# Graph convolutions: 28 of 56 tiles gathered and seven groups picked, in place of 24 and eight, with the scan's flags in PSUM

## What is computed

```python
edge_index = jnp.stack([src, dst])
x = _layernorm(x + L0(x, edge_attr_16, ...))    # edge softmax over incoming edges
x = _layernorm(x + L1(x, edge_type_8, ...))     # two relational convolutions
x = _layernorm(x + L2(x, edge_attr_8, ...))     # message and update products
x = _layernorm(x + L3(x, edge_attr_8, ...))     # three edge-conditioned convolutions

# one relational convolution (L1)
msg = sum over r of where(edge_type == r, x[src] @ W[r], 0)
out = segment_sum(msg * norm[:, None], dst) + x @ root + bias

# one edge-conditioned convolution (L3)
W = (edge_attr @ ew + eb).reshape(E, 16, 16)
msg = einsum('ei,eio->eo', x[src], W)
out = segment_sum(msg, dst) + x @ rw + rb
```

## Time and profile before

| | us |
|---|---|
| median of three runs | 13711.05 (13693.49 to 13768.67) |
| profiled execution, own time | 13760.25 |
| its span | 13759.0 |
| stretch of r0 | 1150 |
| stretch of r1 | 1368 |
| stretches of c0, c1, c2 | 1490, 1512, 1503 |
| granted TensorE clock, mean | 0.786 |

### The profile page before, as it was taken

The page is one execution under the profiler, slowest core; times in us unless marked ns, Lnnn a source line. Parts: engine busy times, 40 slices in busy tenths (PEclk is TensorE's granted clock), DMA queues, the critical chain, the costliest instruction groups (busy, mean ns, idle before and its releaser), DMA issues. The chain is left out here.

```text
span 13759.0 us, 163456 instructions
## 1 busy us (share of the span) xinstructions
PE 10347.0 (75%) x42305; PEld 7078.4 (51%) x42305; DVE 9334.6 (68%) x14722; ACT 8279.7 (60%) x16314; POOL 7292.7 (53%) x6233
## 2 busy tenths in 40 slices
PE   6888888888724887687748888777775777767775
PEld 2333333333313665565537777655554555545554
DVE  8999999999878776343349999545554454535454
ACT  5777777777623665465538887455553555535553
POOL 4555555555653776555457776344443444444444
PEclk7666666666657998798879999788886888778887
DMA  3444444444434776465521111266664666546663
GB/s 129 176 177 177 176 179 178 177 176 176 159 125 170 255 255 214 140 205 184 187 62 46 45 45 44 58 207 212 206 210 127 203 203 203 190 138 213 202 207 124
DMA packets 750356, 2256.00 MB, mean 164 GB/s; under 512 B 272537, under 2 KB 420654, under 8 KB 673806
## 3 DMA queue, kind: packets, MB, share of 16 engines
q10 hardware_dynamic: 161280, 1027.68, 21.8%
q1 hardware_dynamic: 388638, 984.49, 19.0%
q0 software_dynamic: 200304, 242.20, 8.0%
HBM read 1321.84 MB, written 931.93 MB: 164 GB/s over the span
## 5 line engine op out<-in xcount | busy, mean ns | idle before, releaser
L592 POOL DMA_INDIRECT h<-in_x,idx x1568 | 2055.3, 1311 | 1699.8 <-DMA efT<-in_edge_attr_t 1245.4
L676 ACT ACTIVATE PX<-PX,h 128x16 f32<-128x16 f32 x12544 | 2513.1, 292 | 23.0 <-issue 13.8
L1474 PE MATMUL PS<-every_weight,dstf 112*128 112x144 f32 (+1 forms) x8960 | 1444.3, 302 | 625.7 <-DVE dstf L1606 387.5
L1474 PEld LDWEIGHTS PS<-every_weight,dstf 112*128 112x128 f32 x8960 | 1338.8, 206 | 843.4 <-DVE dstf L1606 409.0
L625 PE MATMUL PS<-M,minus_ident 128*128 128x512 f32 x1568 | 1410.2, 1025 | 310.0 <-DVE M L710 310.0
L1992 PE MATMUL PS<-mhr,lhs 128*128 128x392 f32 x6272 | 1264.6, 358 | 204.1 <-DVE lhs L2156 193.1
L1959 POOL DMA_INDIRECT myg<-node_table,mix x784 | 1099.9, 1403 | 458.7 <-issue 247.0
L2055 ACT ACTIVATE mhr<-mhb 128x1568 fp32r<-128x1568 bf16 x784 | 1142.2, 1505 | 302.6 <-DVE mhb L2146 251.9
L1992 PEld LDWEIGHTS PS<-mhr,lhs 128*128 128x128 f32 x6272 | 1151.9, 194 | 291.8 <-ACT mhr L2055 141.1
L613 PE MATMUL PS<-waug,efT 17*128 17x256 f32 x6272 | 1038.7, 534 | 283.4 <-DVE e L688 247.7
L1452 POOL DMA_INDIRECT c0yg<-node_table,c0ix x672 | 686.1, 1021 | 950.6 <-DVE c0run L1675 555.3
(11 more groups left out here) (419 smaller groups left out, 20474.8 us busy)
## 6 DMA issues: line engine op xcount, KB each, us to landing
softmax_maxima<-M SPq DMA_DIRECT2D x196, 1024.0 KB
softmax_denominators<-ST SPq DMA_DIRECT2D x196, 1024.0 KB
softmax_numerators<-ST SPq DMA_DIRECT2D x196, 1024.0 KB
one_hot_rows_of_sources<-r0hb ACTq DMA_DIRECT2D x224, 896.0 KB
r1hb<-one_hot_rows_of_sources ACTq DMA_DIRECT2D x224, 896.0 KB
c0hb<-one_hot_rows_of_sources ACTq DMA_DIRECT2D x224, 896.0 KB
c1hb<-one_hot_rows_of_sources ACTq DMA_DIRECT2D x224, 896.0 KB
c2hb<-one_hot_rows_of_sources ACTq DMA_DIRECT2D x224, 896.0 KB
```

Source lines behind the costliest of these rows:

```text
L592: PO.indirect_dma_start(h[b.k][:, at(q), :], None, io["x"], bass.IndirectOffsetOnAxis(ap=idx[b.k][:, q:q + 1], axis=0))\
L676: act = S.activation(PX[b.k][:, 1, t, D * i:D * i + D], PX[b.k][:, 0, t, D * i:D * i + D], ACT.Copy, scale=h[b.k][:, t, i:i + 1])
L1474: mm = PE.matmul(weighed(q)[:, r, 0:R * D], mx[q % (1 + LAG)][:, 128 * r:128 * r + 128], every[0:A9 * D, 0:R, :].rearrange("p r o -> p (r ...
```

## The change

NG goes from 24 to 28 and HG from 8 to 7, so a block has 28 gathered tiles and 28 picked ones. With it:

- c0 to c2 scale seven groups of gathered tiles instead of six. The first round of `halve` goes over seven tiles at a time (eight pieces a block) instead of eight (seven pieces); in r0 and r1 it stays at four pieces, of seven tiles instead of eight.
- In c0 to c2 DVE calls `add_both` four times a step instead of three, in two pairs, and `mask` stands between the pairs instead of behind them. The messages of the first 28 tiles are k = 14, in step 3.
- `kp`, the scan's flags, is one array in PSUM banks 2 and 3 instead of two in SBUF. `keeps` now waits for the scan of the block before instead of the one before that.
- As HG is odd, PSUM banks, `hot_` and `mx` alternate by a running count (`turn_of`, `masked`). Buffer 3 of the ring is used once a block, and its load for the next block goes ahead of those of buffers 0 to 2.
- The stored one-hot rows are contiguous for each group.
- In r0 the one-hots of a block fill three and a half buffers, and are spread as four a step.

```diff
-NG, HG = 24, 8
+NG, HG = 28, 7
-            NSC, NTR = (6, 13) if both else (0, 6)
+            NSC, NTR = (7, 14) if both else (0, 6)
...
-                    kp.append(sb(f"{name}kp{k}", [CH, D, TBC], F32, L))
+                    kp.append(PS[0:CH, 2:4, :].rearrange("p b c -> p (b c)")[:, 0:D * TBC].rearrange("p (f t) -> p f t", f=D))
...
+            def turn_of(b, q):
+                return (b.k * HG + q) % 2
+
+            def masked(b, q):
+                return mx[(b.k * HG + q) % (1 + LAG)]
...
             def rows(b, half, from_):
-                return from_[some(b, NG + 16 * half, 16), :].rearrange("(a t) c -> a (t c)", a=1).to_broadcast([128, 2048])
+                n = min(16, NPK - 16 * half)
+                return from_[some(b, NG + 16 * half, n), :].rearrange("(a t) c -> a (t c)", a=1).to_broadcast([128, 128 * n])
...
-                if due(n := groups(b, q - 3)):
+                if due(n := groups(b, (-2, -1, 0, -3, 1, 2, 3)[q])):
                     S.wait_ge(*h_cv.at(n))
...
                 def keeps(b):
-                    if due(n := b.on(-2).count(1, 1)):
+                    if due(n := b.on(-1).count(1, 1)):
...
-                            load_rows(nx, p + 4)
+                            load_rows(nx, (4, 5, 6, HG + 3, HG, HG + 1, HG + 2)[p])
...
-                    at = 1024 * (j % 2)
+                    at, n2 = 1024 * (j % 2), min(2, HG - 2 * j)
...
-                    if nx and n < 3 + p % 2:
-                        one_hot(nx, (p + 3) // 2 if p % 2 else (p + 2) // 2, n if p % 2 else 4 + n)
+                    if nx:
+                        one_hot(nx, (11 + 4 * p + n) // KT, (11 + 4 * p + n) % KT)
...
-                    if k < 6:
+                    if k < 7:
                         scale_gathered(b, k)
...
+                            halve(b, slice(t0 + 7 * n, t0 + 7 * n + 7), 4 * D)
...
-                        if b:
-                            if both:
-                                add_both(b, 3 * p)
-                            else:
-                                add_typed(b, p)
+                        if b and both:
+                            add_both(b, 4 * p)
+                            add_both(b, 4 * p + 1)
+                        elif b:
+                            add_typed(b, p)
                         one_hots(nx, p, 1)
-                        if b and both:
-                            add_both(b, 3 * p + 1)
+                        if both and nx:
+                            mask(nx, p)
                         one_hots(nx, p, 2)
                         if b and both:
-                            add_both(b, 3 * p + 2)
+                            add_both(b, 4 * p + 2)
+                            add_both(b, 4 * p + 3)
```

More of the change, by code:

```diff
@@ L1369, in conv @@
             sums_c = sums[0:E, :].rearrange("(p t) f -> p t f", p=CH)
-            KEPT = 16 * sum(kept(q) for q in TWO)
+            PER = (32, 32, 32, 16)
             def groups(b, more):
@@ L1499, in stored_rows @@
             def stored_rows(b, q):
-                rows = hots_d[bass.ds(b.i * HG + (b.k * (HG // 2) + q // 2), 1), :, q % 2, :, :]
+                rows = hots_d[bass.ds(b.i * (2 * HG) + (b.k * HG + q), 1), :, :, :]
                 return rows.rearrange("a p c e -> (a p) c e")
             def keep_rows(b, q):
-                if make and kept(q):
+                if make:
                     S.dma_start(stored_rows(b, q), hb[q // 2][:, q % 2, :, :]).then_inc(h_ld[q // 2].sem, 16)
@@ L1510, in load_rows @@
                     b, q = b.on(1), q - HG
-                if make or not kept(q) or not b.exists():
+                if make or not b.exists():
                     return
-                if due(n := groups(b, q - 3)):
+                if due(n := groups(b, (-2, -1, 0, -3, 1, 2, 3)[q])):
                     S.wait_ge(*h_cv.at(n))
@@ L1518, in widen @@
                 def widen(b, q):
-                    if make or not kept(q):
+                    if make:
                         S.wait_ge(*h_oh.at(b.count(4 * KT, KT * (q // 2) + KT)))
                     else:
-                        S.wait_ge(*h_ld[q % 4].at(b.count(32, 16 * (q // 4) + 16)))
+                        S.wait_ge(*h_ld[q % 4].at(b.count(PER[q % 4], 16 * (q // 4) + 16)))
                     if due(n := groups(b, q - 1)):
                         S.wait_ge(*h_g.at(n))
-                    S.activation(hot_[q % 2][:, :, :], hb[q // 2 if make else q % 4][:, q % 2 if make else 0, :, :], ACT.Copy)\
+                    S.activation(hot_[turn_of(b, q)][:, :, :], hb[q // 2 if make else q % 4][:, q % 2 if make else 0, :, :], ACT.Copy)\
                         .then_inc(h_cv.sem, 1)
@@ new lines, in add_both @@
+                    elif k < 23:
+                        half, n = (k - 7) // 8, (k - 7) % 8
+                        done, t0 = 7 * half, 28 * half
+                        if n < 4:
+                            if half == 0:
+                                V.wait_ge(*c_sc.at(b.count(NSC, min(2 * n + 2, 7))))
+                            else:
+                                V.wait_ge(*c_pr.at(groups(b, min(2 * n + 2, HG))))
+                            halve(b, slice(t0 + 7 * n, t0 + 7 * n + 7), 4 * D)
+                        elif n < 6:
+                            V.wait_ge(*c_tr.at(b.count(NTR, done + 2 * n - 6)))
+                            halve(b, slice(t0 + 14 * n - 56, t0 + 14 * n - 42), 2 * D)
+                        elif n == 6:
+                            V.wait_ge(*c_tr.at(b.count(NTR, done + 6)))
+                            halve(b, slice(t0, t0 + 28), D)
+                        else:
+                            V.wait_ge(*c_tr.at(b.count(NTR, done + 7)))
+                            if half == 0:
+                                run_free(b)
+                            else:
+                                V.wait_ge(*c_al.at(groups(b, HG)))
+                            ts = slice(t0, t0 + 28)
+                            V.tensor_tensor(by_feature(b, ts), y[:, ts, 0:D], y[:, ts, 8 * D:], ALU.add).then_inc(c_msg.sem, 1)
+                    elif k == 23:
@@ L1689, in add_typed @@
                     elif k < 5:
-                        V.wait_ge(*c_pr.at(groups(b, 2 * k)))
-                        halve(b, slice(8 * k - 8, 8 * k), 4 * D)
+                        V.wait_ge(*c_pr.at(groups(b, min(2 * k, HG))))
+                        halve(b, slice(7 * k - 7, 7 * k), 4 * D)
                     elif k < 7:
@@ L1816, in whole @@
                     of.base += 16 * NBC
-                for of in h_ld:
-                    of.base += 32 * NBC
+                for of, per in zip(h_ld, PER):
+                    of.base += per * NBC
                 for of in c_g:
```

92 lines of the change are left out of this document (33 added, 59 removed).

## The result

The changed kernel takes 14,308.9 us (median of four, 14,292 to 14,387) beside 13,731.6 us for the kernel before: 1.043 times as long, interval 1.040 to 1.046. I had forecast 13,913 us and a range up to 14,130. The profiled execution took 14,319.9 us, 560 more than that of before. About an hour after E1 to E4 and on another chip, the same two kernels took 12,229.5 and 11,632.9 us, 1.051 (1.050 to 1.053). E12 and E13 show why.

What follows compares the result with a forecast made beforehand. No engine is always busy; PE loses about 20 us a block while POOL gathers. c0 to c2 +156, r1 -30, r0 +91, ends -15: +202 on 13,760 us, median 13,913 us (+1.5%), own range 13,790 to 14,060, wider 13,560 to 14,130.

Steps and rivals of the forecast that it cites:

- Bursts: c0 to c2: a block's run of gathers, 28 after the change, 35.8 us; POOL then waits in a gap.
- second kind: c0 to c2: blocks whose next mask comes behind the gathers; 55.5 us against 55.2, three blocks of four.
- the ends: r1 and c0 to c2: two blocks without gathers save a group each, four more gathers precede each: -15 us.
- The step from the scan's hold to the mix: c0 to c2: without the scan delaying gathers, more blocks get their mask late: 54.5 us, +2.0 a block, +156 us.
- fixed stall: Rival: what holds PE costs a fixed 20 us a block, however many gathers; 13,332 us, chance 0.14.
- PE further: Rival: PE gets further while POOL gathers without the scan's help; 13,559 us, chance 0.12.
- Five microseconds of burst cancel a group of 4.2 almost exactly: c0 to c2: longer gathering offsets the group removed; blocks 55.5 against 55.2 us, or 51.5 against 51.6.
- first kind: c0 to c2: blocks with a mask still inside the gathers, 27 to 30 us after their start; 51.5 against 51.6 us.
- PE needs only 7 x 4.2 = 29 us and cannot be the limit unless it crawls: r0: POOL's time alone sets the stage, 41.4 us a block against 38; +91 us.
- r0 falls into r1's pattern: Rival: DVE, waiting for rows, no longer slows r0's gathers; 48 us a block, +196, 14,096 us and up; chance 0.10.
- five masks fall in the first 22 us as now: r1: mask times in the gathers stay, sixth at 40 us; 47.5 us a block against 48.5, stage -30 us.
- the crawl: All stages: PE slows while POOL gathers; in c0 to c2 until some 2.5 us after the last gather.

Runs made afterwards that it cites:

- E1: Kernel before with a small POOL memset (128 x 128, 0.22 us) behind each gather: 13,405 us, 0.974 of before.
- E4: Changed kernel with only the scan's flags moved back to SBUF: 13,450 us, 0.980 of before.
- E12: Kernel before, unchanged, run again with its trace on a chip without the slowdown of PE: 11,633 us.
- E13: Changed kernel, unaltered, run again with its trace beside a before of 11,633 us: 12,230 us, 1.051 of before.
- E3: Kernel before with only the scan's flags moved to PSUM: 14,028 us, 1.022 of before.
- E5: Changed kernel, flags in PSUM, plus a spare scan a block that reads two SBUF arrays: 13,490 us, 1.001 of before.
- E7: Changed kernel with flags in SBUF and the old split (24 gathered, eight groups picked) in r0 and r1: 13,213 us, 0.985 of before.
- E16: Kernel before with only the scan's flags in PSUM, repeated on another chip: 1.019 of before.
- E17: Kernel before with only the scan's flags in PSUM, a third time: 1.018 of before.
- E6: Kernel before with a larger POOL memset (128 x 320, 0.38 us) behind each gather: 12,541 us, 0.933 of before.
- E8: Changed kernel with POOL memsets in place of the gathers, gathered rows left out of the sums: 10,979 us in one execution.

## Why the prediction was wrong

**c0 to c2: right for the changed kernel, in part by luck.** Bursts mostly of 35.7 to 36.3 us (forecast 35.8), each fourth of 37 to 37.6; gaps mostly of 17 to 20 (15 or 19 to 20); 68 of 75 blocks of the second kind (forecast three of four); +180 us for the three stages against +156 less their share of the ends. The step from the scan's hold to the mix, which I had only argued, is shown on the old split: 20 of 75 blocks are of the second kind in before and 67 in E3, and their mean goes from 52.5 to 54.4 us. E5 shows it on the new one. The two rivals that let PE off (fixed stall, PE further) fell. But the two parts of the +180 were mis-sized in opposite directions. "Five microseconds of burst cancel a group of 4.2 almost exactly" put the split alone at nothing, and the lost hold at 2.0 us a block. With E4 (from another group of runs), the split alone is -604 us in the three stages and the flags are +784: a block of the new split with the hold takes 45.1 us and not 52.6. That these errors cancel is luck. The mask inside a burst was misread, too: in the 55 blocks of the first kind in before it falls 14.5 to 31.5 us after the start, in 36 of them under 27, and not at 27 to 30.

**"PE needs only 7 x 4.2 = 29 us and cannot be the limit unless it crawls" failed in r0: +91 us forecast, +261 measured.** I costed r0 as POOL's time alone, because the trace of before shows POOL there nearly without a pause. But the condition was in the sentence and I gave it no price of its own in the sum. In r0, too, PE crawls where nothing holds the gathers; before, DVE's one-hots held them nearly always. Now, in eight blocks, PE is late, DVE has nothing to do, holds nothing, and the gathers run at 1.26 us (27 in 34.0 us); that keeps PE late, until POOL has used up its buffers and waits. The gathers' mean did fall (865.81 / 784 + 0.30 = 1.40 us, forecast 1.48), and the stage got longer: 224 us are POOL's ten waits. This is the rival "r0 falls into r1's pattern"; I gave it 0.10, and priced it at +196 together with +234 in c0 to c2. The split brings most of it (r0 +174 in E4, with flags in SBUF); E7, with the old split in r0, has none of it (1094). Two figures of the sum for r0 do not follow from those beside them (672 x 1.58 + 22 is 1084 and not 1081; 8.0 less 1.2, less an eighth, is 6.0 and not 6.5); they are worth 17 us and decide nothing.

**r1: -30 us forecast, +139 measured.** The step that failed is "five masks fall in the first 22 us as now". Mostly four do, the third at 10 to 15 us and the fourth at 17 to 24, and blocks take mostly 52 us in place of 48. E4 has the same (+152), so the cause is in the split and what comes with it, seven-tile sums or masks' order; which of these, no run tells apart. The size is loose: the old split took 1232 to 1399 us in r1 on four chips or more with the crawl (E3, E16 and E17 are one and the same code), the new one, without memsets, 1457 to 1519.

The sum: the five stages were to take 202 us more, ends included, and took 580 more. Of the 378 us between them r0 is 170, r1 169 and c0 to c2 with the ends 39. Outside the stages the kernel lost 20 us.

**What the prediction could not see.** It took the crawl for a property of the kernel. It is one of the chip's condition at the time. The result fell in the same condition as the trace that I had read, so this is not why the forecast missed. But for what the change is worth it matters: five of seven groups of runs had it, two had not, and one chip was seen in both. Without it the change costs 5.1% by plain arithmetic: POOL sets all five stages, and gets four gathers more a block. c0 to c2 +145, +144 and +146, r1 +103, r0 +50, together 588 of the 597 us. Four gathers of 1.25 us are 140 us in 28 blocks; r1 and r0 lose less because their gathers are held less (means of 1.44 and 1.37 us in r1, 1.58 and 1.42 in r0). So the change is slower either way, for different reasons: with the crawl, because the flags in PSUM take away what held the gathers in c0 to c2 and the split slows r0 and r1; without it, because it adds to the engine that is full. What puts a chip in the one condition or the other, and what stops PE in the crawl, is open.

The crawl also turns signs round. To before, with it and without it: flags in SBUF on the new split 0.980 and 1.067; the memset of 0.38 us 0.933 and 1.067. I have no version that beats before in both. E7 does with the crawl; E6 is the best there.

## What to carry to other kernels

A trace in which an engine stands for "issue" between its instructions, beside transfers, can show a condition of the chip and not the kernel alone; profile the same code again, on another chip and later, before tuning against it. An edit that gains by slowing a neighbour (a hold, a memset) gains only while the slowness is there. Where a sum says "cannot be the limit unless", the clause after "unless" is a rival with a price, above all when the same mechanism was just seen in the stage next to it.

## What the runs showed of the hardware

- PE's pace beside gathers has two conditions. In one, unheld gathers every 1.25 us leave PE 34 matmuls in 34 us; with a memset behind each (every 1.335 us) part of the stages crawl, and with a longer one (every 1.495 us) none. In the other, 24 unheld gathers every 1.25 us go with 118 matmuls in 29.3 us, and groups of 4.21 us.
- POOL memsets of 128 x 128, 128 x 224 and 128 x 320 took 0.22, 0.32 and 0.38 to 0.40 us. No run showed PE slowed by them.
- A gather took 0.94 us beside a scan with one of its two inputs in PSUM, and up to 2.73 us beside one with both in SBUF.
- With no gathers at all (E8) the kernel took 10,979 us, 1,250 less than the changed kernel's 12,230 without the crawl. The two are from different groups of runs, and E8 has memsets in place of the gathers, so this is an estimate of what gathering costs.
